# Layer 1 attention of a two-layer post-norm network: q and k turned in fp32 two heads at a time and split behind the turn, scores in 64-row tiles, row maximum written negated

## The chip, the cores and the metric

The kernel runs on one core of a Trainium2 chip. The metric is the device time of one execution in microseconds, from the first instruction to the last. Lower is better. Three executions of the kernel before took 630.36, 634.5 and 637.96 us, median 634.5.

A core has four engines that compute, each with its own in-order queue: TensorE (PE in the profile, its weight loads PEld), VectorE (DVE), ScalarE (ACT) and GpSimd (POOL). SyncE (SP) issues transfers. Engines wait for each other through semaphores. TensorE writes to PSUM, which has eight banks of 128 x 512 fp32 values here.

## The reference, cut to what matters

Two layers, each an attention and a feed-forward part with residual and layer norm, on x of shape (2, 512, 256). The change concerns the attention of layer 1: 32 query heads and 8 key/value heads of 64 values, so four query heads share a key head, rotary embedding, RMS norm of q and k, and a causal window of 64 positions.

```python
q, k, v = split(x @ w_qkv.T)           # 32, 8 and 8 heads of 64
q, k = rms_norm(q) * q_norm_w, rms_norm(k) * k_norm_w
q, k = q * cos + rot_half(q) * sin, k * cos + rot_half(k) * sin
scores = q @ k.T / sqrt(64)            # kept where 0 <= q_pos - k_pos < 64
out = softmax(scores) @ v
y = out @ w_out.T
```

The result is fp32. The kernel keeps its precision in TensorE's fast fp32r type by splitting a value into a high part, rounded to fp32r, and a low part, the remainder, and summing high x high, high x low and low x high.

## The kernel before

One program list, `STEPS`, sets the order of the work on every engine. Each engine's block walks through the list and does its own part of each step, so an instruction is never moved past one ahead of it in its queue. The order is: layer 0 attention, layer 0 feed-forward (`ffn`), layer 1 attention, layer 1 feed-forward.

**Passes.** Layer 1 attention works on 16 items, one for each batch and key head (`NIT`). It is a software pipeline of 22 passes. In pass n an engine does the steps of its list (`TENSOR_PASS`, `SCALAR_PASS`, `VECTOR_PASS`, `GPSIMD_PASS`), and an entry (name, behind, part) works on item n - behind. Three passes are done early, inside the layer 0 feed-forward. Passes 16 to 21 also carry the weight chunks of layer 1's feed-forward.

**An item** goes through these steps:
- `proj1` (x times w_qkv, four tiles t of 128 rows). PE writes 384 columns, and ScalarE copies them to `qkv_rows` (L853); VectorE copies tile 0 (L1143).
- `squares` on ScalarE, `square_sums` on VectorE (L1104), `rms_inverses` on GpSimd (L1281, L1282).
- `cosines` on VectorE (L1098), `sines` on GpSimd (two products, L1273), `rope_sums` on VectorE (L1111), which also tells GpSimd that `rope_sin_part` is free for the next sines. `normed` multiplies by the inverse and writes `roped` (L1120).
- `rows_high` on ScalarE (L889, L890) and `rows_low` on GpSimd (L1256, L1259) split q and k while positions are still on the partitions.
- `turn1k`, `turn1q` turn them on PE with an fp32r identity (L581): high and low of one head stand side by side, so one turn gives the high in rows 0 to 63 and the low in rows 64 to 127. ScalarE copies q to `q_stack` (L871) and k's high part twice into `k_stack` (L866, L867); VectorE copies k's low part twice (L1129, L1130).
- `scores1(k, c)`, c = 0 to 3: a bank first gets the mask (64-row bf16 matmul, L607), then eight matmuls over 128 rows (L616), which sum high and low of q against k's high and k's low.
- `maxima` on VectorE: a reduction (L1147), and a product by -1/8 of its 128x4 result (L1148) behind a wait for the first. `exps` on ScalarE: four exponentials with scale 1/8 and bias `minus_max`, each with its row sum (L877).
- `probs` on VectorE: reciprocal (L1135) and product (L1136). `turn_p` on PE (L624) with a copy on ScalarE (L894). `pv1` on PE (L638), ScalarE takes the high part (L899), VectorE the low (L937).
- `out1` on PE with w_out (L391 to L393); `wout` splits the chunk of w_out on ScalarE (L781) and GpSimd (L1228).

**Banks.** `claim` hands out banks 0 to 5 in a ring and makes PE wait until the bank's former contents have been read.

Of the kernel before, what the change touches and what calls it, by code (L numbers as in the profile page):

```python
# [1396 lines left out]
```

## Time and profile before

| | |
|---|---|
| three executions | 630.36, 634.5, 637.96 us |
| profiled execution | 634.5 us, span of its instructions 634.5 us |
| PE busy | 573.6 us (90%) |
| VectorE busy | 471.7 us (74%) |
| ScalarE busy | 385.9 us (61%) |
| GpSimd busy | 326.3 us (51%) |
| mean granted TensorE clock | 0.925 |

Busy time is the union of an engine's instructions. For matmuls it is a rough figure: they are pipelined and each record contains its latency. The granted clock is the share of TensorE's 2.4 GHz, and it has two levels, 1.0 and 0.5 (1.2 GHz). From about 200 to 545 us the kernel is in the layer 1 attention.

### The profile page before, as it was taken

How to read it: one execution, taken by the hardware profiler on the slowest of the kernel's cores; microseconds unless marked ns; L12 is line 12 of the kernel's file. 1: busy time of each engine (PE TensorE's matmuls, PEld its weight loads, DVE VectorE, ACT ScalarE, POOL GpSimd, SP SyncE). 2: the span in 40 equal slices, each digit the busy share in tenths (PEclk: the TensorE clock that was granted, in tenths of full speed). 3: DMA queues.
4: the chain of work that ended last, by engine and by line, in shares of the span. 5: the costliest groups of instructions: out<-in, count | busy, mean ns of one | idle time of the engine just before them, and what ended most of it. 6: DMA issues, size and time to landing. Idle time of an engine off the chain costs nothing.

```text
span 634.5 us, 11068 instructions
## 1 busy us (share of the span) xinstructions
PE 573.6 (90%) x3912; PEld 480.4 (76%) x3912; DVE 471.7 (74%) x786; ACT 385.9 (61%) x1020; POOL 326.3 (51%) x197
## 2 busy tenths in 40 slices
PE   3687988899999689999999999799999999899994
PEld 3444664688889678888888898688987787788883
DVE  4757777674455899999999999989998753363444
ACT  2555666415344378888888888758886665532230
POOL 2868665303423986666876666565759431230000
PEclk9878999899999788999999999989996765999997
DMA  8211001041310000000000000001011001000010
GB/s 305 77 38 33 3 1 34 2 147 54 92 33 1 1 1 18 1 19 18 18 19 18 2 18 19 18 1 35 18 35 51 27 24 52 34 1 1 1 34 33
DMA packets 8886, 21.10 MB, mean 33 GB/s; under 512 B 1280, under 2 KB 2944, under 8 KB 8704
## 3 DMA queue, kind: packets, MB, share of 16 engines
q1 hardware_dynamic: 8832, 20.40, 9.9%
q8 instruction: 32, 0.52, 0.3%
q14 instruction: 22, 0.18, 0.1%
HBM read 19.35 MB, written 1.05 MB: 32 GB/s over the span
## 4 chain that ended last, share of the span: by engine, by line
PE 45%; DVE 35%; issue 9%; ACT 4%; POOL 3%; DMA 1%; DVEq 1%; POOLq 0%; SPq 0%; ACTq 0%
PE psum L391 9%; PE psum L393 9%; PE psum L392 9%; DVE row_max L1147 5%; PE psum L616 4%; DVE rope_cos_part L1098 3%; DVE square_sums L1104 3%; DVE rope_cos_part L1111 3%; DVE roped L1120 3%; PE psum L467 3%; DVE probs L1136 3%; PE psum L450 2%; DVE out_t_low L937 2%; PE psum L638 2%; DVE minus_max L1148 2%
## 5 line engine op out<-in xcount | busy, mean ns | idle before, releaser
L877 ACT ACTIVATE probs<-psum,minus_max 128x128 f32<-128x128 f32 x256 | 90.5, 368 | 33.5 <-DVE minus_max L1148 33.4
L1273 POOL TENSOR_TENSOR rope_sin_part<-qkv_rows,sin_weighted 128x640 f32<-128x640 f32 x32 | 67.1, 2114 | 81.1 <-DVE rope_cos_part L1111 67.5
L616 PEld LDWEIGHTS psum<-k_stack,q_stack 128*128 128x128 f32 x512 | 71.6, 216 | 16.8 <-issue 16.8
L616 PE MATMUL psum<-k_stack,q_stack 128*128 128x128 f32 (+1 forms) x512 | 81.2, 308 | 0.0
L1282 POOL TENSOR_TENSOR rms_inverse<-rms_inverse,minus_half 128x20 f32<-128x20 f32 x16 | 58.7, 3668 | 1.3
L1237 POOL TENSOR_TENSOR weights_t<-weights_t,causal_block 128x512 f32<-128x512 f32 x32 | 45.3, 1437 | 23.7 <-DVE weights_t L981 18.6
L848 ACT CAST hidden_high<-hidden 128x512 fp32r<-128x512 f32 x32 | 19.8, 620 | 60.7 <-DVE hidden L1059 60.7
L1147 DVE TENSOR_REDUCE row_max<-psum 128x4 f32<-128x512 f32 x64 | 43.6, 682 | 12.9 <-PE psum L616 12.5
L877 ACT ACTIVATION_READ_ACCUMULATOR probs<-psum,minus_max 128x1 f32 x256 | 52.7, 206 | 0.0
L391 PE MATMUL psum<-x_t_high,ug_high 128*128 128x512 f32 x128 | 51.5, 402 | 0.0
L392 PE MATMUL psum<-x_t_low,ug_high 128*128 128x512 f32 x128 | 50.8, 396 | 0.0
L393 PE MATMUL psum<-x_t_high,ug_low 128*128 128x512 f32 x128 | 50.7, 396 | 0.0
L1148 DVE TENSOR_SCALAR minus_max<-row_max 128x4 f32<-128x4 f32 x64 | 47.0, 734 | 2.2
L1250 POOL TENSOR_SCALAR ln_var_eps<-ln_mean_var 128x4 f32<-128x4 f32 x8 | 1.8, 227 | 90.4 <-DVE ln_mean_var L1016 90.4
L391 PE MATMUL psum<-qkv_high,x_t_high 128*128 128x384 f32 x128 | 47.4, 371 | 0.5 <-DVE out_t_low L937 0.5
L1136 DVE TENSOR_TENSOR probs<-probs,prob_inverse 128x512 f32<-128x512 f32 x64 | 44.3, 692 | 2.2
L393 PE MATMUL psum<-qkv_high,x_t_low 128*128 128x384 f32 x128 | 44.1, 345 | 0.0
L392 PE MATMUL psum<-qkv_low,x_t_high 128*128 128x384 f32 x128 | 44.1, 345 | 0.0
L391 PE MATMUL psum<-wout_high,out_t_high 128*128 128x256 f32 x128 | 39.7, 310 | 3.5 <-DVE x_rows L1010 3.5
L624 PE MATMUL psum<-identity,probs 128*128 128x128 f32 x256 | 39.0, 288 | 3.9 <-DVE probs L1136 2.4
L581 PE MATMUL psum<-identity_r,q_rows_high_low 128*128 128x128 f32 x256 | 35.7, 281 | 6.3 <-DVE k_stack L1130 5.1
L1256 POOL TENSOR_TENSOR q_rows_high_low<-roped,q_rows_high_low 128x1024 fp32r<-128x1024 f32 x16 | 39.2, 2450 | 2.9 <-ACT k_rows_high_low L890 2.8
(159 smaller groups left out, 1667.5 us busy)
## 6 DMA issues: line engine op xcount, KB each, us to landing
raw_chunks<-in_ug SPq DMA_DIRECT2D x8, 512.0 KB, 3.6
raw_chunks<-in_wout SPq DMA_DIRECT2D x16, 256.0 KB, 2.7
raw_chunks<-in_qkv SPq DMA_DIRECT2D x8, 384.0 KB, 3.2
raw_chunks<-in_x SPq DMA_DIRECT2D x2, 512.0 KB, 5.1
raw_chunks<-in_w SPq DMA_DIRECT2D x2, 512.0 KB, 5.8
raw_chunks<-in_sel SPq DMA_DIRECT2D x2, 512.0 KB, 7.1
down_tree<-in_down SPq DMA_DIRECT2D x1, 1024.0 KB, 9.2
x_rows<-in_x_rows SPq DMA_DIRECT2D x2, 512.0 KB, 5.7
```

Source lines behind the costliest of these rows:

```text
L391: nc.tensor.matmul(o, ah_, bh_, start=first, stop=False, **kw)
L392: nc.tensor.matmul(o, ah_, bl_, start=False, stop=False, **kw)
L393: return nc.tensor.matmul(o, al_, bh_, start=False, stop=last, **kw)
L616: mm = nc.tensor.matmul(o[:, at:at + k1 - k0], qst[:, hp, qb, :], kst[:, k % 2, z, k0:k1], start=False, stop=z == 1, skip_group_check=True)
L877: e = nc.scalar.activation(pr[:, c, q, :], o[:, q * P:(q + 1) * P], ACT.Exp, bias=negm[:, c, q:q + 1], scale=float(HD1) ** -0.5, accum_out ...
L1136: nc.vector.tensor_tensor(pr[:, c], pr[:, c], pinv[:, c, :].rearrange("p (q a) -> p q a", a=1).to_broadcast([P, 4, P]), ALU.mult).then_inc ...
L1147: link(nc.vector.tensor_reduce(mx[:, c, :], o.rearrange("p (q w) -> p q w", q=4), AX.X, ALU.max))
L1148: nc.vector.tensor_scalar(negm[:, c, :], mx[:, c, :], -float(HD1) ** -0.5, None, ALU.mult).then_inc(mx_done[c], 1)
L1237: nc.gpsimd.tensor_tensor(w, w, tri[:].rearrange("p (a q) -> p a q", a=1).to_broadcast([P, HG, P]), ALU.mult).then_inc(w_mask, 1)
L1256: nc.gpsimd.tensor_tensor(qhl[:, :, :, 1, :], qn[:, :, 0:REP * HD1].rearrange("p t (h d) -> p t h d", h=REP), qhl[:, :, :, 0, :].bitcast(F ...
L1273: last = nc.gpsimd.tensor_tensor(ov[:, :, :, z, :], rv[:, :, :, 1 - z, :], sv[:, :, :, z, :], ALU.mult)
L1282: nc.gpsimd.tensor_tensor(r, r, half[:], ALU.pow).then_inc(rr_done, 1)
```

## The change

Where q and k are split changes. `normed` now writes k twice side by side (so `roped` has 384 values for each row instead of 320) in a first operation, and q in a second. PE turns these fp32 rows directly, two heads in one transpose, with k's turn giving k in both row halves. Only behind the turn are they split, ScalarE writing the high part (fp32r) and VectorE the low part, by subtraction from PSUM. `rows_high` and `rows_low` are gone.

`scores1` now has two parts instead of four. Each fills two banks, one for each of the two heads of a pair, from rows 0 to 63 and from rows 64 to 127, with three matmuls (high-high, high-low, low-high) over 64 rows. The factor 1/8 moves from the exponential to the tables for q. The reduction for the row maximum writes the negated maximum directly, so the 128x4 product is gone. `proj1(0, 0)`'s copy moves from VectorE to ScalarE. The order of the steps in all four lists is new.

```diff
+GN = GW + HD1
-TENSOR_PASS = [("turn1k", 4), ("out1", 6, 0), ("turn_p", 5, 0), ("turn_p", 5, 1), ("turn1q", 4, 0),
-    ("turn_p", 5, 2), ("proj1", 1, 1), ("turn1q", 4, 1), ("turn1q", 4, 2), ("turn1q", 4, 3), ("turn_p", 5, 3),
-    ("scores1", 4, 0), ("pv1", 5, 0), ("scores1", 4, 1), ("proj1", 1, 2), ("scores1", 4, 2), ("scores1", 4, 3),
-    ("out1", 6, 1), ("pv1", 5, 1), ("proj1", 1, 3), ("proj1", 0, 0)]
-SCALAR_PASS = [("turn1k", 4), ("squares", 2), ("turn_p", 5, 0), ("turn_p", 5, 1), ("turn1q", 4, 0), ("turn_p", 5, 2),
-    ("proj1", 1, 1), ("turn1q", 4, 2), ("turn1q", 4, 1), ("turn1q", 4, 3), ("turn_p", 5, 3), ("wout", 5),
-    ("rows_high", 3), ("pv1", 5, 0), ("exps", 4, 0), ("proj1", 1, 2), ("exps", 4, 1), ("exps", 4, 2), ("pv1", 5, 1),
-    ("exps", 4, 3), ("proj1", 1, 3)]
-VECTOR_PASS = [("turn1k", 4), ("probs", 5, 3), ("values1", 2), ("rope_sums", 3), ("normed", 3), ("maxima", 4, 0),
-    ("square_sums", 2), ("maxima", 4, 1), ("maxima", 4, 2), ("pv1", 5, 0), ("cosines", 2), ("maxima", 4, 3),
-    ("probs", 4, 0), ("probs", 4, 1), ("probs", 4, 2), ("pv1", 5, 1), ("proj1", 0, 0)]
-GPSIMD_PASS = [("rms_inverses", 3), ("sines", 2), ("wout", 5), ("rows_low", 3)]
+TENSOR_PASS = [("turn1k", 4), ("turn1q", 4, 0), ("turn1q", 4, 1), ("turn_p", 5, 0), ("turn_p", 5, 1), ("out1", 6, 0),
+    ("proj1", 1, 1), ("scores1", 4, 0), ("pv1", 5, 0), ("turn_p", 5, 2), ("turn_p", 5, 3), ("proj1", 1, 2),
+    ("scores1", 4, 1), ("out1", 6, 1), ("pv1", 5, 1), ("proj1", 1, 3), ("proj1", 0, 0)]
+SCALAR_PASS = [("turn1k", 4), ("turn1q", 4, 0), ("turn1q", 4, 1), ("turn_p", 5, 0), ("turn_p", 5, 1), ("squares", 2),
+    ("proj1", 1, 1), ("exps", 4, 0), ("pv1", 5, 0), ("exps", 4, 1), ("turn_p", 5, 2), ("turn_p", 5, 3), ("wout", 5),
+    ("proj1", 1, 2), ("exps", 4, 2), ("pv1", 5, 1), ("exps", 4, 3), ("proj1", 1, 3), ("proj1", 0, 0)]
+VECTOR_PASS = [("turn1k", 4), ("turn1q", 4, 0), ("turn1q", 4, 1), ("probs", 5, 3), ("values1", 2), ("square_sums", 2),
+    ("maxima", 4, 0), ("maxima", 4, 1), ("pv1", 5, 0), ("rope_sums", 3), ("probs", 4, 0), ("normed", 3),
+    ("probs", 4, 1), ("maxima", 4, 2), ("maxima", 4, 3), ("pv1", 5, 1), ("cosines", 2), ("probs", 4, 2)]
+GPSIMD_PASS = [("rms_inverses", 3), ("sines", 2), ("wout", 5)]
...
             def turn1k(k):
-                pe.wait_ge(identr_set, 1)
-                pe.wait_ge(rows_hi, k + 1)
-                pe.wait_ge(rows_lo, k + 1)
+                pe.wait_ge(qn_done, k + 1)
                 o, done = claim(("turn1k", k))
                 for t in range(TT):
-                    mm = turned(o[:, t * P:(t + 1) * P], khl[:, t, :, :])
+                    mm = nc.tensor.transpose(o[:, t * P:(t + 1) * P], qn[:, t, REP * HD1:GN], ident[:])
                 mm.then_inc(done, 1)
-            def turn1q(k, t):
-                o, done = claim(("turn1q", k, t))
-                for h in range(REP):
-                    mm = turned(o[:, h * P:(h + 1) * P], qhl[:, t, h, :, :])
+            def turn1q(k, hp):
+                o, done = claim(("turn1q", k, hp))
+                for t in range(TT):
+                    mm = nc.tensor.transpose(o[:, t * P:(t + 1) * P], qn[:, t, hp * P:(hp + 1) * P], ident[:])
                 mm.then_inc(done, 1)
...
+                banks = [claim(("scores1", k, 2 * half_ + h2)) for h2 in range(2)]
+                rows = [slice(HD1 * h2, HD1 * (h2 + 1)) for h2 in range(2)]
+                for h2 in range(2):
+                    nc.tensor.matmul(banks[h2][0], eye2[rows[h2], :], wmask[rows[h2], half_, :], start=True, stop=False,
+                                     skip_group_check=True)
+                emptied(pe, ("turn1k", k), ("turn1q", k, 0), ("turn1q", k, 1))
+                n = k % 2
+                for q4 in range(4):
+                    qb = 4 * half_ + q4
+                    k0, k1 = max(0, (qb - 1) * WIN), (qb + 1) * WIN
+                    at = q4 * P + P - (k1 - k0)
+                    for z, (qt, kt) in enumerate(((qth, kth), (qth, ktl), (qtl, kth))):
+                        for h2 in range(2):
+                            o, done = banks[h2]
+                            mm = nc.tensor.matmul(o[:, at:at + k1 - k0], qt[rows[h2], n, qb, :, :].rearrange("p a w -> p (a w)"),
+                                                  kt[rows[h2], n, k0:k1], start=False, stop=z == 2,
+                                                  skip_group_check=True)
...
+                high(("turn1k", k), kth[:, k % 2, :])
...
+                nc.scalar.copy(qth[:, k % 2, :, hp, :], o.rearrange("p (qb w) -> p qb w", qb=NQ)).then_inc(hi_done, 1)
...
             def normed(k):
...
-                    dve.wait_ge(rows_lo, k)
+                    filled(dve, ("turn1k", k - 1))
+                    for hp in range(2):
+                        filled(dve, ("turn1q", k - 1, hp))
+                inverse = rr[:, k % 2, :].rearrange("p (t h a) -> p t h a", t=TT, a=1)
                 nc.vector.tensor_tensor(
-                    qn[:].rearrange("p t (h d) -> p t h d", d=HD1), rot1[:].rearrange("p t (h d) -> p t h d", d=HD1),
-                    rr[:, k % 2, :].rearrange("p (t h a) -> p t h a", t=TT, a=1).to_broadcast([P, TT, REP + 1, HD1]),
-                    ALU.mult).then_inc(qn_done, 1)
+                    qn[:, :, REP * HD1:GN].rearrange("p t (a d) -> p t a d", a=2),
+                    rot1[:, :, REP * HD1:GW].rearrange("p t (a d) -> p t a d", a=1).to_broadcast([P, TT, 2, HD1]),
+                    inverse[:, :, REP:REP + 1, :].to_broadcast([P, TT, 2, HD1]), ALU.mult)
+                nc.vector.tensor_tensor(
+                    qn[:, :, 0:REP * HD1].rearrange("p t (h d) -> p t h d", d=HD1),
+                    rot1[:, :, 0:REP * HD1].rearrange("p t (h d) -> p t h d", d=HD1),
+                    inverse[:, :, 0:REP, :].to_broadcast([P, TT, REP, HD1]), ALU.mult).then_inc(qn_done, 1)
...
+                low(("turn1k", k), ktl[:, k % 2, :], kth[:, k % 2, :])
+            def turn1q(k, hp):
+                low(("turn1q", k, hp), qtl[:, k % 2, :, hp, :], qth[:, k % 2, :, hp, :],
+                    lambda o: o.rearrange("p (qb w) -> p qb w", qb=NQ))
...
-                link(nc.vector.tensor_reduce(mx[:, c, :], o.rearrange("p (q w) -> p q w", q=4), AX.X, ALU.max))
-                nc.vector.tensor_scalar(negm[:, c, :], mx[:, c, :], -float(HD1) ** -0.5, None,
-                                        ALU.mult).then_inc(mx_done[c], 1)
+                nc.vector.tensor_reduce(negm[:, c, :], o.rearrange("p (q w) -> p q w", q=4), AX.X, ALU.max,
+                                        negate=True).then_inc(mx_done[c], 1)
```

## Rows read from the trace of the kernel before

**Rows 1.** Busy time, five even passes: PE, PEld, DVE, ACT, POOL, PEclk, DMA, GB/s.

```profile
280.68:376.30 95.62, 95.03 (x763) 83.91 (x761) 93.26 (x140) 80.34 (x256) 66.77 (x35) 1.00 0.05 15
```

**Rows 2.** VectorE's groups, 280.68 to 376.30: count, busy us, mean ns, idle before.

```profile
L1148 DVE TENSOR_SCALAR minus_max<-row_max 128x4 f32<-128x4 f32 x20 | 16.5, 824 | 0.7
L1136 DVE TENSOR_TENSOR probs<-probs,prob_inverse 128x512 f32<-128x512 f32 x20 | 13.8, 692 | 0.7
L1147 DVE TENSOR_REDUCE row_max<-psum 128x4 f32<-128x512 f32 x20 | 13.6, 680 | 0.2
...
L1120 DVE TENSOR_TENSOR roped<-rope_cos_part,rms_inverse 128x1280 f32<-128x1280 f32 x5 | 7.5, 1492 | 0.2
...
L937 DVE TENSOR_TENSOR out_t_low<-psum,out_t_high 128x512 fp32r<-128x512 f32 x10 | 6.8, 680 | 0.0
L1130 DVE CAST k_stack<-psum 64x512 fp32r<-64x512 f32 x5 | 3.5, 694 | 0.1
...
L1143 DVE COPY qkv_rows<-psum 128x384 f32<-128x384 f32 x5 | 2.7, 546 | 0.0
```

**Rows 3.** VectorE in order of time, one pass: start us, us, what.

```profile
280.68 1.49 DVE L1111 TENSOR_TENSOR rope_cos_part<-rope_cos_part,rope_sin_part 128x1280 f32<-128x1280 f32 x1
...
288.51 1.72 DVE L1148 TENSOR_SCALAR minus_max<-row_max 128x4 f32<-128x4 f32 x1
...
292.95 0.17 DVE L1135 RECIPROCAL prob_inverse<-prob_sums 128x4 f32<-128x4 f32 x1
...
293.77 0.17 DVE L1135 RECIPROCAL prob_inverse<-prob_sums 128x4 f32<-128x4 f32 x1
...
299.81 1.49 DVE L1111 TENSOR_TENSOR rope_cos_part<-rope_cos_part,rope_sin_part 128x1280 f32<-128x1280 f32 x1
```

**Rows 4.** ScalarE in order of time, the same pass.

```profile
284.99 0.58 ACT L899 CAST out_t_high<-psum 128x512 fp32r<-128x512 f32 x1
285.47 0.37 ACT L877 ACTIVATE probs<-psum,minus_max 128x128 f32<-128x128 f32 x1
...
286.85 0.49 ACT L853 COPY qkv_rows<-psum 128x384 f32<-128x384 f32 x1
```

**Rows 5.** GpSimd in order of time, the same pass.

```profile
282.34 4.28 POOL L1273 TENSOR_TENSOR rope_sin_part<-qkv_rows,sin_weighted 128x640 f32<-128x640 f32 x2 [5.54 <-DVE rope_cos_part L1111]
286.58 1.27 POOL L1228 TENSOR_TENSOR wout_low<-raw_chunks,wout_high 128x512 fp32r<-128x512 f32 x1
287.82 2.38 POOL L1256 TENSOR_TENSOR q_rows_high_low<-roped,q_rows_high_low 128x1024 fp32r<-128x1024 f32 x1
```

**Rows 6.** VectorE in order of time, an early pass.

```profile
208.71 2.79 DVE L1120 TENSOR_TENSOR roped<-rope_cos_part,rms_inverse 128x1280 f32<-128x1280 f32 x1 [0.73 <-POOL rms_inverse L1282]
```

**Rows 7.** GpSimd in order of time, the same early pass.

```profile
208.58 4.33 POOL L1273 TENSOR_TENSOR rope_sin_part<-qkv_rows,sin_weighted 128x640 f32<-128x640 f32 x2
```

**Rows 8.** VectorE in order of time, in layer 0.

```profile
25.52 3.41 DVE L956 TENSOR_TENSOR x_t_low<-raw_chunks,x_t_high 128x1024 fp32r<-128x1024 f32 x1 [2.22 <-ACT x_t_high L781]
```

**Rows 9.** GpSimd in order of time, in layer 0.

```profile
25.49 2.34 POOL L1204 TENSOR_TENSOR down_tree<-down_tree 128x1024 f32<-128x1024 f32 x1
```

**Rows 10.** PE in order of time, layer 0 scores, 64-row matmuls in both row halves.

```profile
89.83 0.76 PE L450 MATMUL psum<-qk_stacks 64*128 64x512 f32 x4
90.52 1.71 PE L467 MATMUL psum<-weights_t,v_and_ones 128*32 128x512 f32 x16
```

**Rows 11.** PE in order of time, the same pass as Rows 3.

```profile
281.17 1.11 PE L616 MATMUL psum<-k_stack,q_stack 128*128 128x64 f32 x8
...
298.15 1.11 PE L581 MATMUL psum<-identity_r,q_rows_high_low 128*128 128x128 f32 x9
```

**Rows 12.** The chain that ended last, in the tail: start us, us, what.

```profile
499.65 0.70 DVE k_stack L1130
...
523.42 0.71 DVE k_stack L1130
```

**Rows 13.** Busy time by stages, in the tail; columns as in Rows 1.

```profile
503.00:507.00 4.00, 4.00 (x26) 3.44 (x25) 2.24 (x1) 0.67 (x2) 2.90 (x2) 0.50 0.01 3
```

More of the change, by code:

```diff
@@ L227, in post_ln_two_layers @@
         with ExitStack() as s:
-            qn = place(s, "roped", [TT, GW], F32)
-            qhl = place(s, "q_rows_high_low", [TT, REP, 2, HD1], F32R)
-            khl = place(s, "k_rows_high_low", [TT, 2, HD1], F32R)
+            qn = place(s, "roped", [TT, GN], F32)
             wol = place(s, "wout_low", [2, 2, C], F32R)
-            qst = place(s, "q_stack", [2, NQ, P], F32R)
-            kst = place(s, "k_stack", [2, 2, T], F32R)
+            qth = place(s, "q_t_high", [2, NQ, 2, WIN], F32R)
+            qtl = place(s, "q_t_low", [2, NQ, 2, WIN], F32R)
+            kth = place(s, "k_t_high", [2, T], F32R)
+            ktl = place(s, "k_t_low", [2, T], F32R)
             pr = place(s, "probs", [4, 4, P], F32)
@@ new lines, in scores1 @@
+                for q4 in range(4):
[8 more added lines that the diff above has]
+                                                  skip_group_check=True)
+                            if q4 == 3 and z == 2:
+                                mm.then_inc(done, 1)
@@ L862, in turn1k @@
             def turn1k(k):
-                o, _ = take(act, ("turn1k", k))
-                hi_no["turn1k", k] = len(hi_no) + 1
-                nc.scalar.copy(kst[0:HD1, k % 2, 0, :], o[0:HD1])
-                nc.scalar.copy(kst[HD1:P, k % 2, 0, :], o[0:HD1]).then_inc(hi_done, 1)
-            def turn1q(k, t):
-                o, done = take(act, ("turn1q", k, t))
-                nc.scalar.copy(*to_qst(o, t)).then_inc(done, 1)
+                high(("turn1k", k), kth[:, k % 2, :])
+            def turn1q(k, hp):
+                o, _ = take(act, ("turn1q", k, hp))
+                hi_no["turn1q", k, hp] = len(hi_no) + 1
+                nc.scalar.copy(qth[:, k % 2, :, hp, :], o.rearrange("p (qb w) -> p qb w", qb=NQ)).then_inc(hi_done, 1)
             def exps(k, c):
@@ L1069, in rope_tables @@
                     for t in range(TT):
-                        last = nc.vector.tensor_tensor(
-                            tab[:, t, :].rearrange("p (h d) -> p h d", h=REP + 1),
-                            nw[:, z, :].rearrange("p (h d) -> p h d", h=REP + 1),
-                            ctab[:, z, t, :].rearrange("p (a d) -> p a d", a=1).to_broadcast([P, REP + 1, HD1]),
-                            ALU.mult)
+                        angle = ctab[:, z, t, :].rearrange("p (a d) -> p a d", a=1)
+                        for h0, h1, by in ((0, REP, float(HD1) ** -0.5), (REP, REP + 1, 1.0)):
+                            cols = slice(h0 * HD1, h1 * HD1)
+                            last = nc.vector.scalar_tensor_tensor(
+                                out=tab[:, t, cols].rearrange("p (h d) -> p h d", d=HD1),
+                                in0=nw[:, z, cols].rearrange("p (h d) -> p h d", d=HD1), scalar=by,
+                                in1=angle.to_broadcast([P, h1 - h0, HD1]), op0=ALU.mult, op1=ALU.mult)
                 last.then_inc(tabs_done, 1)
@@ L1155, in pv1 @@
                     lambda o: o.rearrange("p (q hp w) -> p q hp w", q=4, hp=2))
-            in_pass = dict(proj1=proj1, turn1k=turn1k, pv1=pv1, maxima=maxima, probs=probs, cosines=cosines,
+            in_pass = dict(turn1k=turn1k, turn1q=turn1q, pv1=pv1, maxima=maxima, probs=probs, cosines=cosines,
                            square_sums=square_sums, normed=normed, values1=values1, rope_sums=rope_sums)
@@ L1171, in tree_step @@
             def tree_step():
-                for name in ("identity", "scale_ug", "scale_dp"):
+                for name in ("scale_ug", "scale_dp"):
                     dve.wait_ge(const_in[name], 16)
-                nc.vector.tensor_copy(identr[:], ident[:]).then_inc(identr_set, 1)
                 nc.vector.tensor_scalar(scale_ug[:], scale_ug[:], float(C) ** -0.5, None, ALU.mult)
```

75 lines of the change are left out of this document (13 added, 62 removed).

## The prediction, made before the changed kernel ran

> **What bounds the kernel now.** I read the busy time by stages first, then VectorE's groups in the layer 1 attention, then one pass of that stage engine by engine. The stage is a software pipeline of 22 passes. Between 280.68 and 376.30 us five passes run alike at the full TensorE clock, 19.12 us each, VectorE busy 93.26 of 95.62 us and PE 95.03 [rows 1]; the same step of VectorE, `rope_sums`, starts at 280.68 and 299.81 [rows 3]. The reader should see two engines without slack, ScalarE at 80.3 and GpSimd at 66.8. PE's busy time counts overlapping records, so it is an upper bound.
>
> Then one oddity: `minus_max`, a 128x4 operation, takes 0.824 us on average, more than a reduction of 128x512 at 0.680 [rows 2]. At 288.51 it takes 1.72 us, until GpSimd's operation that began at 287.82 and took 2.38 is over [rows 3, 5]. So some VectorE operations with both ends in SBUF wait until a running GpSimd operation is through. A `tensor_tensor` with two SBUF inputs does too: `roped`, 1.49 us otherwise, took 2.79 when GpSimd's sine product had started 0.13 us before it [rows 2, 6, 7], and a split at 25.52 took 3.41 because GpSimd had started at 25.49 [rows 8, 9]. In the first of these the two sine products took 4.33 us. Free of waits they take about 2.9: in the even pass 4.28 us, of which the first 1.36 (282.34 to 283.70) are under `roped` [rows 5]. So in the early pass they alternated: product, `roped`, product [rows 6, 7]. Reductions and PSUM operands show no such wait.
>
> **VectorE, per pass.** From 19.12 us go four `minus_max`, 4 x 0.824 = 3.30; the copy of `proj1(0,0)`, 0.55 (ScalarE takes it); two `k_stack` casts, 1.39. Added are three subtractions PSUM minus SBUF; their like is `out_t_low` at 0.680, of which some 0.07 overlaps the next: +1.85. `normed` becomes 128x512 and 128x1024: 0.69 and, between 0.69 for 512 and 1.49 for 1280, 1.23, less overlap, against 1.49: +0.3 [rows 2]. Work left: 16.0 us.
>
> But the queue order adds waits. ScalarE now runs `exps(0)` before the high part of `pv1(0)`, and VectorE's `pv1` low part stands right behind `maxima(0)`, `maxima(1)`. From the end of the first maximum: 0.09 to the exponentials, 1.38 for four of them (285.47 to 286.85), 0.58 for the high part, together 2.05 us [rows 4]; VectorE has only the second maximum, 0.60, to fill it. Idle 1.45 us. The same pattern comes again with `maxima(2)`, `maxima(3)`: 2.9 us a pass, so 18.9. In the kernel before, the first high part goes ahead of the exponentials, and VectorE has three `probs` ahead of the second low part.
>
> Then the port. `rope_sums` is now followed by `probs(0)`, `normed` (two operations), `probs(1)`: four products of two SBUF inputs in a row. `rope_sums` also releases GpSimd's two sine products, and `wout_low` (1.27 us [rows 5]) is queued behind them. Before, `roped` stood there alone and was first in. Now a reciprocal comes first (0.17 us; reciprocal and product together move the queue on by 0.82, from 292.95 to 293.77 [rows 3]), so the product starts some 0.23 us behind the end of `rope_sums`. GpSimd starts 0.17 behind it: 282.34 against 280.68 + 1.49 [rows 3, 5]. I take it that they alternate: VectorE waits about 1.35, 1.4 and 1.15 us for the three GpSimd operations: 3.9 us. Bounds: nothing, if VectorE is first and keeps the port over consecutive operations; 4.3, the three whole. I take 3.9, as the one row where both waited shows alternation. VectorE's pass: 16.0 + 2.9 + 3.9 = 22.8 us, **3.7 us more**. The rope tables take eight operations more and the identity copy is gone, both in layer 0, where VectorE has gaps: 0, and 2 to 3 us without them.
>
> The Trainium skill, "SBUF — State Buffer", section on SBUF's two separate sides, calls the shared pair an exclusive lock, granted for the whole instruction to whoever starts first. It doesn't say who gets it when both wait; with VectorE keeping it the sum would be that of the second rival.
>
> **PE.** The turn of q falls from 16 matmuls (nine take 1.11 us [rows 11]) to 8 transposes, k stays at 4: about -0.9. The scores: 32 matmuls at 0.13 us (eight take 1.11 with the last one's latency [rows 11]) become 48 on 64 rows. Half-height matmuls in the two row halves run at the same time: four of 512 columns take 0.69 us to the next group, 0.17 each, under the 0.21 that 512 columns need at 2.4 GHz [rows 10]. So 24 pairs at 0.11 to 0.13, about 2.9 instead of 4.2, and masks in pairs, -0.6. From 19.0 PE falls to some 16.3 us, under VectorE; if halves did not overlap, it would be 19, still under 22.8. This is hidden.
>
> **ScalarE and GpSimd.** ScalarE loses four `q_stack`, two `k_stack` and two row casts and gains three casts and a copy, so its 16.1 us can only fall; GpSimd loses `rows_low`, whose larger part takes 2.38 us [rows 5]. Both lie beside VectorE: 0. If VectorE had no waits, PE would be next.
>
> **A queue of banks.** Claims go round six banks, 17 to a pass. The last turn of q may only be written once `exps(3)` of the pass before is done; from there PE has turns 0.5, two turns of probabilities 1.0, `out1` 1.4, `proj1` 1.1, scores 1.8: 5.8 us at full clock. VectorE gets to its first maximum about 6.7 us behind `exps(3)`. Hidden by 0.9 us.
>
> **Sum.** Passes 5 to 16 are of this kind: 12 x 3.7 = +44. Pass 4: +3. In the tail (no projections) `k_stack` comes at 499.65 and 523.42, 23.8 us apart [rows 12], PE at half clock between (0.50 at 503 to 507 [rows 13]). There eight scores matmuls take about 1.9, and the new scores save some 3 us of PE. Pass 17 keeps all of VectorE's work: 22.8, no gain; pass 18 about 21, -3; pass 19 about 16, -6: -9. 634.5 + 44 + 3 - 9 = 672.5, forecast **672 us**. The profiled execution's 634.5 is also the median of the three runs, which spread from 630.4 to 638.0, so within 1% (6 us) nothing can be told from no change.
>
> **Rivals.**
> 1. *The clock falls in every pass* (slower still). Waiting for `exps(3)` behind a late `maxima(3)`, PE stands about 4 us. The clock fell in the tail after a stand between the q turns. At half clock for part of PE's 5.8 us path, 2.5 more less the 0.9 in hand: +1.6 on 13 passes, 693 us. For: the longer stand. Against: in the five even passes it never fell with as many projections. Chance 0.15. The Trainium skill, "TensorE: Matmul & The Clock Gate", Part 4, says that transposes don't count as activity for the clock; 20 in a row now open a pass. The trace doesn't separate this.
> 2. *VectorE keeps the port, or gets there first.* 18.9 us a pass: 13 x -0.2 = -3, and the tail -13 (pass 17 gains 3 and pass 18 4 instead of 0 and 3): **618 us**, the other side. It decides at the start of `probs(0)`: if that starts ahead of the sine product, this holds. For: the starts lie only 0.06 us apart by estimate. Against: the alternation, and 25.49 against 25.52. Chance 0.16.
> 3. *Only the first sine product blocks.* 18.9 + 1.4 = 20.3: +1.2 x 13 = 15, tail -11: 638. Chance 0.16.
> 4. *The waits of step order don't bind either*, and the pass is the busiest engine's 16.4: -2.7 x 13 = -35, tail -13: 587. For: the work really is removed. Against: in-order queues, and both waits are certain by the rows. Chance 0.10.
>
> **Chances and range.** My case 0.43. Faster by over 1% (under 628): rivals 2 and 4 and a little of 3, 0.28. Within 1%: most of 3, 0.14. Slower: 0.58. The range leaves out rival 4 and the outer half of the first and goes from 612 to 698; the likeliest case alone is 660 to 685 (a pass of 21.8 to 23.8).
>
> **What would show it.** A pass of 22 to 24 us between consecutive `rope_sums`. `probs` on average well above 0.69 us and the two parts of `roped` near 2.1 and 2.4; `minus_max` straight from PSUM at 0.68. VectorE idle about 1.45 us ahead of `out_t_low`, twice a pass, released by ScalarE. Score matmuls starting in pairs, thousandths of a us apart. In the tail, passes under 22 us. I am wrong if `probs` stays at 0.69 (rival 2), if only the first of each pass is long (rival 3), or if VectorE has no waits ahead of `out_t_low` (rival 4); the granted clock between 280 and 376 us tells rival 1.

## The result and the profile after

The kernel after the change takes **686.1 us** (median of four executions, 678.8 to 688.5), the kernel before 633.0 (median of four, 630.4 to 638.0): ratio 1.081, 95% interval 1.073 to 1.089. It is slower, as forecast; 672 had been predicted, in a range of 612 to 698. The profiled execution took 688.5 us, its span is 686.7. Some executions of one kernel ran over 1.5% longer than its fastest, at a lower granted clock (three of nine for e2, five of ten for e4 below), and medians and ratios leave them out.

First the busy time of the page, and below it the same for four passes of the stage, to be set beside [rows 1]:

```profile
PE 556.4 (81%) x4040; PEld 473.3 (69%) x4040; DVE 477.6 (70%) x745; ACT 345.1 (50%) x956; POOL 278.5 (41%) x165
```

```profile
301.60:397.01 95.41, 76.10 (x640) 68.68 (x640) 77.31 (x101) 54.35 (x190) 41.23 (x20) 0.86 0.04 12
```

The stretch is as long as before but holds four passes instead of five: 23.88 us each against 19.12. No engine is full any more: PE is busy for 76.1 of 95.4 us and VectorE for 77.3, of which, as the next rows show, 3.6 us a pass are waits inside its operations. Work went, waits came. VectorE's groups in that stretch (count, busy us, mean ns, idle before and who ended it) answer to [rows 2]:

```profile
L1116 DVE TENSOR_TENSOR probs<-probs,prob_inverse 128x512 f32<-128x512 f32 x16 | 14.6, 912 | 0.5
L1100 DVE TENSOR_TENSOR roped<-rope_cos_part,rms_inverse 128x1024 f32<-128x1024 f32 x4 | 10.3, 2567 | 0.0
L1122 DVE TENSOR_REDUCE minus_max<-psum 128x4 f32<-128x512 f32 x16 | 10.3, 681 | 3.3 <-PE psum L606 3.3
L1096 DVE TENSOR_TENSOR roped<-rope_cos_part,rms_inverse 128x512 f32<-128x512 f32 x4 | 8.2, 2047 | 0.0
L908 DVE TENSOR_TENSOR out_t_low<-psum,out_t_high 128x512 fp32r<-128x512 f32 x9 | 6.2, 692 | 14.3 <-ACT out_t_high L870 14.3
...
L908 DVE TENSOR_TENSOR k_t_low<-psum,k_t_high 128x512 fp32r<-128x512 f32 x4 | 2.8, 692 | 1.3 <-ACT k_t_high L751 1.3
```

Two things are to be seen: `probs` and both parts of `roped` are long, and 14.3 us of idle stand ahead of nine `out_t_low`. One pass of VectorE in order of time (start us, us, what; in brackets the idle before and its releaser) shows both. It answers to [rows 3].

```profile
349.26 1.48 DVE L1084 TENSOR_TENSOR rope_cos_part<-rope_cos_part,rope_sin_part 128x1280 f32<-128x1280 f32 x1
350.66 0.17 DVE L1115 RECIPROCAL prob_inverse<-prob_sums 128x4 f32<-128x4 f32 x1
350.86 0.69 DVE L1116 TENSOR_TENSOR probs<-probs,prob_inverse 128x512 f32<-128x512 f32 x1
351.47 2.05 DVE L1096 TENSOR_TENSOR roped<-rope_cos_part,rms_inverse 128x512 f32<-128x512 f32 x1
353.44 2.57 DVE L1100 TENSOR_TENSOR roped<-rope_cos_part,rms_inverse 128x1024 f32<-128x1024 f32 x1
...
356.13 1.58 DVE L1116 TENSOR_TENSOR probs<-probs,prob_inverse 128x512 f32<-128x512 f32 x1
357.63 1.28 DVE L1122 TENSOR_REDUCE minus_max<-psum 128x4 f32<-128x512 f32 x2
360.48 0.69 DVE L908 TENSOR_TENSOR out_t_low<-psum,out_t_high 128x512 fp32r<-128x512 f32 x1 [1.58 <-ACT out_t_high L870]
...
363.72 0.69 DVE L908 TENSOR_TENSOR k_t_low<-psum,k_t_high 128x512 fp32r<-128x512 f32 x1 [0.33 <-ACT k_t_high L751]
...
369.65 1.29 DVE L1122 TENSOR_REDUCE minus_max<-psum 128x4 f32<-128x512 f32 x2 [0.85 <-PE psum L606]
372.52 0.69 DVE L908 TENSOR_TENSOR out_t_low<-psum,out_t_high 128x512 fp32r<-128x512 f32 x1 [1.59 <-ACT out_t_high L870]
373.13 1.48 DVE L1084 TENSOR_TENSOR rope_cos_part<-rope_cos_part,rope_sin_part 128x1280 f32<-128x1280 f32 x1
```

GpSimd in the same pass, the answer to [rows 5]:

```profile
350.91 4.02 POOL L1236 TENSOR_TENSOR rope_sin_part<-qkv_rows,sin_weighted 128x640 f32<-128x640 f32 x2 [13.37 <-ACT probs_t L865]
354.88 2.27 POOL L1200 TENSOR_TENSOR wout_low<-raw_chunks,wout_high 128x512 fp32r<-128x512 f32 x1
```

Read the two together. `probs` starts at 350.86, the sine product at 350.91. From then on the engines take turns: `roped` for k takes 2.05 instead of .69, `roped` for q 2.57 instead of 1.23, `probs(1)` 1.58 instead of .69, and GpSimd's operations are stretched too. This is what the prediction calls the port, and VectorE's price is 1.36 + 1.34 + .89 = 3.6 us a pass. The idles are 1.58 and 1.59 ahead of `out_t_low`, .85 ahead of the first maximum, .33 ahead of `k_t_low`. VectorE is busy for 19.3 us of a pass, which is 15.7 without the waits: 15.7 + 3.6 + 3.2 + .85 + .33 = 23.7, against the measured 23.88. The rest are small gaps between operations.

ScalarE shows why `out_t_low` is late (answer to [rows 4]): four exponentials, from 358.40, stand ahead of the cast.

```profile
358.40 0.37 ACT L859 ACTIVATE probs<-psum,minus_max 128x128 f32<-128x128 f32 x1 [6.58 <-DVE minus_max L1122]
...
359.79 0.60 ACT L870 CAST out_t_high<-psum 128x512 fp32r<-128x512 f32 x1
```

PE, finally. The score matmuls start two at a time, .11 us apart. And PE stands for 2.81 us ahead of the first turn of q, until `exps(2)` (from 358.40 to 359.90) gives its bank back, and .77 ahead of the second, until `exps(3)` has:

```profile
350.48 0.29 PE L606 MATMUL psum<-k_t_high,q_t_low 64*128 64x128 f32 x2
350.60 0.29 PE L606 MATMUL psum<-k_t_high,q_t_high 64*128 64x128 f32 x2
...
359.96 1.12 PE L586 MATMUL psum<-identity,roped 128*128 128x128 f32 x4 [2.81 <-ACT probs L859]
361.85 1.11 PE L586 MATMUL psum<-identity,roped 128*128 128x128 f32 x4 [0.77 <-ACT probs L859]
```

The granted clock is 0.86 in this stretch, where it was 1.00 before [rows 1]: in each pass it is at the lower level for 6.8 us, from about the end of that stand on.

**Where the 52 us are.** The `probs` of block 3 comes once in each pass, soon after its start. The first, the thirteenth and the last of the 16, first those of the kernel after, then those of before:

```profile
247.75 0.69 DVE L1116 TENSOR_TENSOR probs<-probs,prob_inverse 128x512 f32<-128x512 f32 x1
...
537.41 0.69 DVE L1116 TENSOR_TENSOR probs<-probs,prob_inverse 128x512 f32<-128x512 f32 x1
...
600.45 0.69 DVE L1116 TENSOR_TENSOR probs<-probs,prob_inverse 128x512 f32<-128x512 f32 x1
```

```profile
240.83 0.69 DVE L1136 TENSOR_TENSOR probs<-probs,prob_inverse 128x512 f32<-128x512 f32 x1
...
478.35 0.69 DVE L1136 TENSOR_TENSOR probs<-probs,prob_inverse 128x512 f32<-128x512 f32 x1
...
549.56 0.69 DVE L1136 TENSOR_TENSOR probs<-probs,prob_inverse 128x512 f32<-128x512 f32 x1
```

Up to the first: +6.9 us. The next twelve gaps: 289.7 against 237.5, +52.1. The last three gaps and the rest of the span: -6.9. Together 52.2 before rounding, which is 686.7 - 634.5.

Of these, 2.2 us are already there when layer 0 ends: its last `hidden` starts at 201.18 us, and at 199.01 before. That is no effect of the change that could be told. In the profiled executions of e1 to e3 and e5 to e10 below, whose layer 0 is that of the kernel after, the same operation starts anywhere between 194.01 (e9) and 201.27 us (e1), with a mean granted clock over the first 100 us of 0.95 in the early ones and 0.88 in the late ones. So differences of whole times of single executions hold up to 7 us of this, and passes are the better measure.

### The profile page after: what moved, and what is told of

Read it like the earlier page. It is cut to its first block and busy times, and to the rows that moved or that the text cites. A ratio compares the mean times of both kernels' runs of the same rounds, so it can differ in the third digit from the quotient of the medians.

```text
span 686.7 us, 11172 instructions
## 1 busy us (share of the span) xinstructions
PE 556.4 (81%) x4040; PEld 473.3 (69%) x4040; DVE 477.6 (70%) x745; ACT 345.1 (50%) x956; POOL 278.5 (41%) x165
## 3 DMA queue, kind: packets, MB, share of 16 engines
HBM read 19.35 MB, written 1.05 MB: 30 GB/s over the span
## 5 line engine op out<-in xcount | busy, mean ns | idle before, releaser
L586 PE MATMUL psum<-identity,roped 128*128 128x128 f32 x128 | 31.0, 398 | 39.0 <-ACT probs L859 39.0
L908 DVE TENSOR_TENSOR out_t_low<-psum,out_t_high 128x512 fp32r<-128x512 f32 x36 | 24.8, 691 | 54.2 <-ACT out_t_high L870 53.9
L1116 DVE TENSOR_TENSOR probs<-probs,prob_inverse 128x512 f32<-128x512 f32 x64 | 56.3, 880 | 2.2
L616 PE MATMUL psum<-identity,probs 128*128 128x128 f32 x256 | 48.2, 348 | 7.2 <-ACT probs L859 7.2
L586 PEld LDWEIGHTS psum<-identity,roped 128*128 128x128 f32 x128 | 21.7, 202 | 45.8 <-ACT probs L859 45.8
L838 ACT COPY qkv_rows<-psum 128x384 f32<-128x384 f32 x64 | 32.2, 506 | 33.7 <-PE psum L388 20.9
L1122 DVE TENSOR_REDUCE minus_max<-psum 128x4 f32<-128x512 f32 x64 | 41.0, 681 | 11.3 <-PE psum L606 11.3
L616 PEld LDWEIGHTS psum<-identity,probs 128*128 128x128 f32 x256 | 40.3, 183 | 11.6 <-issue 11.5
L386 PE MATMUL psum<-wout_high,out_t_high 128*128 128x256 f32 x128 | 46.8, 366 | 0.0
L606 PE MATMUL psum<-k_t_high,q_t_high 64*128 64x128 f32 (+1 forms) x256 | 41.7, 314 | 5.8 <-DVE q_t_low L908 5.8
```

What stands on the lines that cost most here:

```text
L386: nc.tensor.matmul(o, ah_, bh_, start=first, stop=False, **kw)
L586: mm = nc.tensor.transpose(o[:, t * P:(t + 1) * P], qn[:, t, hp * P:(hp + 1) * P], ident[:])
L606: mm = nc.tensor.matmul(o[:, at:at + k1 - k0], qt[rows[h2], n, qb, :, :].rearrange("p a w -> p (a w)"), kt[rows[h2], n, k0:k1], start=Fals ...
L616: mm = nc.tensor.transpose(o[:, q * P:(q + 1) * P], pr[:, c, q, :], ident[:])
L1116: nc.vector.tensor_tensor(pr[:, c], pr[:, c], pinv[:, c, :].rearrange("p (q a) -> p q a", a=1).to_broadcast([P, 4, P]), ALU.mult).then_inc ...
L1122: nc.vector.tensor_reduce(negm[:, c, :], o.rearrange("p (q w) -> p q w", q=4), AX.X, ALU.max, negate=True).then_inc(mx_done[c], 1)
```

## The experiments

Ten kernels. All ratios are to the kernel before, run beside them (medians 633.1 to 634.1 us). A pass is counted from one `rope_sums` to the next, in the stretch from about 301 to 397 us of one profiled execution.

| kernel | median us | ratio, 95% interval | pass us |
|---|---|---|---|
| after | 686.1 | 1.081 [1.073, 1.089] | 23.88 |
| e1: high part of pv1 first | 645.0 | 1.021 [1.015, 1.027] | 20.16, one 21.51 |
| e2: rope_sums early | 635.6 | 1.005 [1.000, 1.010] | 20.5 to 20.6 |
| e3: e1 and e2 | 644.0 | 1.019 [1.012, 1.026] | 20.8 to 22.1 |
| e4: before, maximum negated | 619.9 | 0.978 [0.973, 0.984] | 18.3 to 18.7 |
| e5: after, clock kept up | 675.7 | 1.068 [1.063, 1.074] | 22.92 |
| e6: VectorE's order | 610.1 | 0.963 [0.958, 0.968] | 18.2 to 18.6 |
| e7: scores not paired | 687.7 | 1.087 [1.082, 1.091] | 22.9 to 24.5 |
| e9: e6, wout high later | 608.5 | 0.960 [0.955, 0.965] | 18.4 to 18.6 |
| e8: e9, probs(3) earlier | 605.2 | 0.956 [0.950, 0.963] | 17.8 to 18.6 |
| e10: e8, wout elsewhere | 601.0 | 0.947 [0.939, 0.955] | 17.2 to 18.5 |

### The two waits, one by one

**e1** changes ScalarE's list:

```
-    ("exps", 4, 0), ("pv1", 5, 0), ("exps", 4, 1),  ...  ("exps", 4, 2), ("pv1", 5, 1), ("exps", 4, 3)
+    ("pv1", 5, 0), ("exps", 4, 0), ("exps", 4, 1),  ...  ("pv1", 5, 1), ("exps", 4, 2), ("exps", 4, 3)
```

> The changed kernel with one move on ScalarE alone: in each half pass the high part of pv1 stands ahead of the exponentials instead of behind the first four. My theory: VectorE's two stands of 1.6 us ahead of out_t_low (3.2 us of a pass of 23.9) go, the port waits of 3.6 us stay: a pass of 20.5 to 21.2 us, 645 to 655 us in all. Rival, PE's half-clock stretch sets the pass: the stand moves to row maxima waiting for the scores, a pass of 22.5 to 23.9, 675 to 686 us.

It took 645.0 us. The idle ahead of `out_t_low` fell to .4 us in ten, `roped` stayed at 2.05 and 2.57. The idle of 3.2 us went, and with it, in all passes of the stretch but one, the .85 ahead of the first maximum; the idle ahead of `k_t_low` grew from .33 to .93. Sum: 23.88 - 3.2 - .85 + .6 = 20.4, measured 20.16; an operation that starts without an idle also overlaps the one before it by some .08 us, three times here. The idle that the prediction had counted is real and was on the path.

**e2** changes VectorE's list:

```
-    ("values1", 2), ("square_sums", 2), ("maxima", 4, 0), ("maxima", 4, 1), ("pv1", 5, 0), ("rope_sums", 3), ("probs", 4, 0),
+    ("values1", 2), ("rope_sums", 3), ("square_sums", 2), ("maxima", 4, 0), ("maxima", 4, 1), ("pv1", 5, 0), ("probs", 4, 0),
```

> The changed kernel with one move on VectorE alone: rope_sums stands ahead of square_sums, so that the reductions, which read PSUM or one SBUF tensor, run while GpSimd does its two sine products and wout_low. My theory: the port waits in probs and roped (3.6 us a pass) fall to under 1 us, the stands ahead of out_t_low stay at 3.2: a pass of 20.8 to 21.5, 650 to 658 us. Rival, the products are slow for another reason (their shape, or the k rows written twice): roped stays at 1.9 and 2.5 us and nothing changes, 686.

It took 635.6 us, less than the 650 to 658 expected. `roped` fell to .69 and 1.22, its time without waits, and one `probs` of four kept 1.56 us, beside `wout_low`. So 2.7 of the 3.6 us of port waits went, and the .85 ahead of the first maximum too, because VectorE comes to it later: 23.88 - 2.7 - .85 = 20.3, measured 20.47. `rope_sums` also first runs at 201.4 us instead of 212.3. Of these 10.9 us, 6.6 are layer 0, which was quicker in this execution (its last `hidden` at 194.55). The other 4.3 are the order, and this I had left out. In the kernel after, the second `square_sums` stands ahead of it and waits for GpSimd's power:

```profile
201.18 0.75 DVE L1030 SCALAR_TENSOR_TENSOR hidden<-psum,scale_ug,silu_gate 128x512 f32<-128x512 f32 x1 [6.26 <-PE psum L388]
...
210.89 1.49 DVE L1077 TENSOR_REDUCE square_sums<-squares 128x20 f32<-128x1280 f32 x1 [2.92 <-POOL rms_inverse L1245]
212.30 1.48 DVE L1084 TENSOR_TENSOR rope_cos_part<-rope_cos_part,rope_sin_part 128x1280 f32<-128x1280 f32 x1
```

**e3** does both.

> Both moves at once (high part of pv1 ahead of the exponentials, rope_sums ahead of square_sums). My theory: VectorE keeps 16 us of work and about 1 us of waits, PE needs 16.3 and stands less, so the clock stays up more: a pass of 17 to 18.5 us, 595 to 615 us in all, faster than both kernels. Rival, the clock still falls once a pass: 19 to 20 us, 625 to 640.

A miss, by 29 us and more: 644.0 us, slower than e2 alone and above even the 625 to 640 of its rival. No port wait is left (`probs` .692 on average), yet the pass takes 20.8 to 22.1. ScalarE, then VectorE, of this kernel in order of time:

```profile
310.90 1.11 ACT L865 COPY probs_t<-psum 128x512 f32<-128x512 f32 x2
311.84 0.69 ACT L766 CAST wout_high<-raw_chunks 128x512 fp32r<-128x512 f32 x1
312.36 0.55 ACT L838 COPY qkv_rows<-psum 128x384 f32<-128x384 f32 x1
317.06 0.59 ACT L870 CAST out_t_high<-psum 128x512 fp32r<-128x512 f32 x1 [4.15 <-PE psum L628]
```

```profile
313.15 1.29 DVE L1122 TENSOR_REDUCE minus_max<-psum 128x4 f32<-128x512 f32 x2
317.75 0.69 DVE L908 TENSOR_TENSOR out_t_low<-psum,out_t_high 128x512 fp32r<-128x512 f32 x1 [3.31 <-ACT out_t_high L870]
```

PE of the same stretch:

```profile
311.19 0.39 PE L595 MATMUL psum<-window_mask,eye_twice 64*128 64x512 bf16 x2 [2.81 <-ACT probs L859]
...
315.92 1.09 PE L628 MATMUL psum<-probs_t,v_rows 128*64 128x128 f32 x16
```

Both maxima are done at 314.44, so the exponentials could start by then. But the cast now stands ahead of them, and it waits for pv1's matmuls, which PE starts at 315.92, behind the scores and `out1` that it could not begin before 311.19. ScalarE stands 4.15 us and VectorE 3.31. Some 1.2 us of this is the clock: behind PE's stand of 2.81 us the granted clock is .53 from 313.5 to 316.0, and `out1` takes 2.83 us (from 313.09), where it took 1.62 in the kernel after at the full clock (351.71 to 353.33). e1's cure had cost ScalarE the same kind of stand (29.6 us in ten of them), unseen while VectorE was slow. It moved the wait to ScalarE.

### The part that is a gain by itself

**e4** takes the kernel before and writes the maximum negated, with the factor 1/8 in the tables for q:

```
-                link(nc.vector.tensor_reduce(mx[:, c, :], ..., ALU.max))
-                nc.vector.tensor_scalar(negm[:, c, :], mx[:, c, :], -float(HD1) ** -0.5, None, ALU.mult)...
+                nc.vector.tensor_reduce(negm[:, c, :], ..., ALU.max, negate=True)...
```

> The kernel before with one part of the change: the row maximum is written negated by the reduction, the factor 1/8 moves to the tables of q, and the 128x4 product is gone. VectorE loses 3.7 us of 19.1 a pass. If VectorE alone bounds that kernel: 15.5 to 16.5 a pass, near 600 us. My theory: PE, with some 18.8 us of matmuls, is next at once: 18.7 to 19.0 a pass, 628 to 633. Rival, the port waits pass to the next products of VectorE: no change in VectorE's time, 633 to 636.

Its median is 619.9 us, 2.2% under before (interval 1.6 to 2.7%) and under the 628 to 633 expected. The windows row of five passes, and `cosines` in VectorE's order of time:

```profile
301.60:395.20 93.60, 93.60 (x762) 83.90 (x761) 80.62 (x121) 81.28 (x257) 69.48 (x37) 1.00 0.06 16
```

```profile
305.90 2.26 DVE L1099 TENSOR_TENSOR rope_cos_part<-qkv_rows,cos_weighted 128x1280 f32<-128x1280 f32 x1
```

PE is busy for the whole stretch and VectorE for 80.6 of 93.6 us, with 8.7 us of idle ahead of maxima, waiting for the scores. Here the pass is PE's, at 18.3 to 18.7 us; my estimate of PE's own time before, 19.0, was too high. Of the waits on GpSimd one was handed on: `cosines` takes 2.26 instead of 1.48.

### The clock

**e5** lets PE multiply zeros into the open output accumulator in its stand ahead of the turn of q:

```
             def turn1q(k, hp):
+                if hp == 0 and ... acc1:
...
+                    for _ in range(22):
+                        nc.tensor.matmul(acc1[0][0][:, 0:256], zeros[:, 0:P], zeros[:], start=False, stop=False, ...)
                 o, done = claim(("turn1q", k, hp))
```

> The kernel after, with 22 matmuls of zeros (128x256, bf16) added to the open output accumulator ahead of the turn of the first two q heads, so that TensorE works through its 2.8 us stand of every pass; the output is unchanged. If the half-clock stretch of 6.8 us a pass is what makes the first maximum late (.85 us) and k's low half wait (.33 us), the stretch vanishes and the pass falls from 23.88 to 22.7-22.9: 670-675 us. If the clock lies beside the chain (VectorE's queue alone sets the pass), the clock is kept and the time stays at 684-688. If the added matmuls themselves delay the turns (they are in TensorE's queue), 690-700.

675.7 us, just above the 670 to 675 expected, and a pass of 22.92 as expected: the .96 us is the .85 ahead of the first maximum and little else. Window and maxima of the same stage:

```profile
301.60:393.30 91.70, 83.03 (x742) 76.13 (x743) 76.92 (x101) 54.16 (x188) 40.93 (x21) 0.91 0.04 13
```

```profile
L1129 DVE TENSOR_REDUCE minus_max<-psum 128x4 f32<-128x512 f32 x16 | 10.2, 679 | 0.0
```

The idle ahead of the maxima is 0.0 instead of 3.3 us. The clock still falls at times (0.91), and the .33 ahead of `k_t_low` stays (1.3 us in four). By the medians the slower clock cost 10 us of the 53, by way of late scores. The two profiled executions say 8.7: that much shorter is all that lies behind the first `rope_sums` (465.7 against 474.4 us), and another 3.5 us are layer 0, in which no zeros are multiplied.

### The pairs of score matmuls

**e7** puts the second head's matmuls behind the first's:

```
-                for q4 in range(4): ... for z, (qt, kt) in enumerate(...): for h2 in range(2): <matmul>
+                for h2 in range(2): for q4 in range(4): ... for z, (qt, kt) in enumerate(...): <matmul>
```

> The kernel after, with the score matmuls of the second head all behind those of the first instead of alternating with them; same matmuls, same banks. If the two 64-row tiles of a pair work at once (two matmuls per .11 us), each now takes .11 us or more alone: TensorE +2.6 us a pass, the first head's bank is done as early as before, the second 1.3 us later, of which the first maximum (.6) covers half: +.7 to +1.4 us a pass, 694-702 us. If the pair never ran at once, or the chain has slack there: 684-688.

687.7 us, no change that can be told from 686.1. One head's matmuls alone:

```profile
315.10 0.27 PE L606 MATMUL psum<-k_t_high,q_t_low 64*128 64x128 f32 x1
315.21 0.27 PE L606 MATMUL psum<-k_t_high,q_t_high 64*128 64x128 f32 x1
315.32 0.27 PE L606 MATMUL psum<-k_t_low,q_t_high 64*128 64x128 f32 x1
```

They too start .11 us apart, one where the pair was two. So the two row halves do work at once, and pairing saves about 1.05 us of PE in each half, 2.1 a pass (the 24 take 2.42 us here, from 314.41 to 316.83, and 1.37 in pairs). In the passes it brings nothing, because they are VectorE's: ten of them in a row take 232.8 us here and 232.5 in the kernel after. Outside them the two profiled executions differ, and the equal whole times hide it: layer 0 was 7.0 us shorter in e7's and the part behind the ten passes 5.4 us longer. Two single executions can't say whether the missing pairs have a part in the latter.

### A version that beats both

**e6** fills each idle ahead of `out_t_low` with VectorE's own work and lets GpSimd's sines run beside reductions:

```
-    ("values1", 2), ("square_sums", 2),
-    ("maxima", 4, 0), ("maxima", 4, 1), ("pv1", 5, 0), ("rope_sums", 3), ("probs", 4, 0), ("normed", 3),
-    ("probs", 4, 1), ("maxima", 4, 2), ("maxima", 4, 3), ("pv1", 5, 1), ("cosines", 2), ("probs", 4, 2)]
+    ("values1", 2), ("rope_sums", 3),
+    ("maxima", 4, 0), ("maxima", 4, 1), ("square_sums", 2), ("pv1", 5, 0), ("probs", 4, 0), ("normed", 3),
+    ("probs", 4, 1), ("maxima", 4, 2), ("maxima", 4, 3), ("cosines", 2), ("pv1", 5, 1), ("probs", 4, 2)]
```

> The kernel after, with VectorE's order alone changed: rope_sums ahead of the maxima (so GpSimd's sines run beside maxima and square_sums, which take no part in the port waits), square_sums between the second maximum and out_t_low of half 0, cosines between the fourth maximum and out_t_low of half 1, so that each idle of 1.6 us ahead of out_t_low has VectorE work in it. ScalarE's order stays, so it does not wait for pv1 as it did when its orders were changed. If the pass is VectorE's work plus idle plus port waits, 16.0 + .9 (one probs against wout_low) = 16.9, with TensorE's 16.3 near: pass 17-18.5, 585-610 us, below the 626 of the kernel before with the negated maximum. If a ring through TensorE and ScalarE sets the pass once VectorE is free (as with both changes together, 20.8-22.1): 630-645. If the clock still falls for 3.4 us in a pass: 605-630.

610.1 us: 11% faster than after, by the order of one engine's list alone, and 3.7% faster than before. The pass of 18.5 is longer than the 16.9 of the sum. VectorE's rows show what is left: .89 beside `wout_low`, two idles of up to .5, and 1.2 ahead of `k_t_low`.

```profile
339.33 0.69 DVE L908 TENSOR_TENSOR out_t_low<-psum,out_t_high 128x512 fp32r<-128x512 f32 x1 [0.19 <-ACT out_t_high L870]
...
342.69 1.58 DVE L1116 TENSOR_TENSOR probs<-probs,prob_inverse 128x512 f32<-128x512 f32 x1
```

**e8 and e9** take up the two large ones. Both put ScalarE's wout high one copy later; e8 also moves `probs(3)`:

```
 SCALAR_PASS:
-    ("turn_p", 5, 3), ("wout", 5), ("proj1", 1, 2),
+    ("turn_p", 5, 3), ("proj1", 1, 2), ("wout", 5),
 VECTOR_PASS, e8 alone:
-    ("turn1q", 4, 1), ("probs", 5, 3), ("values1", 2),  ...  ("probs", 4, 2)]
+    ("turn1q", 4, 1), ("values1", 2),  ...  ("probs", 4, 2), ("probs", 4, 3)]
```

> The run before (VectorE's order changed) with two more moves. ScalarE's wout high goes one copy later, so that GpSimd's wout_low starts just after probs(1) instead of just before it (probs(1) took 1.58 against .69: .88 us a pass). And probs of block 3 goes ahead of k's low half, into VectorE's idle of 1.16 us there. If VectorE's queue sets the pass of 18.4-18.6: minus .88 and minus .86, near 16.9-17.3 with TensorE's 16.3 close behind: 588-600 us. If TensorE or a ring through ScalarE takes over at once, 603-611. Above 611 if the later wout high or the earlier turn of probs holds up something else.

> Of these two moves the one of wout high alone. GpSimd and VectorE come for probs(1) within .05 us of each other, so it tells whether the price of .88 us a pass hangs on that order: if VectorE comes first and keeps its .69, the pass falls from 18.5 to 17.6 and the time to 597-602 us; if GpSimd still comes first, no change, 608-612.

e9 came out on the second side of its expectation: 608.5 us, which is e6's within its noise, and the pass stayed. GpSimd, then VectorE:

```profile
339.18 1.29 POOL L1200 TENSOR_TENSOR wout_low<-raw_chunks,wout_high 128x512 fp32r<-128x512 f32 x1 [2.98 <-DVE roped L1100]
```

```profile
339.23 1.79 DVE L1116 TENSOR_TENSOR probs<-probs,prob_inverse 128x512 f32<-128x512 f32 x1
```

GpSimd is still first, by .05 us, and as it has the whole operation before it, `probs` now waits 1.1 instead of .89. e8's second move did work: 17.8 us in most passes, 605.2 us. That is not the 588 to 600 of its theory, and the wait that stayed is 1.1 us a pass of it.

**e10** moves wout right away from those products:

```
 SCALAR_PASS:
-    ("turn1k", 4), ("turn1q", 4, 0), ("turn1q", 4, 1),  ...  ("proj1", 1, 2), ("wout", 5),
+    ("turn1k", 4), ("turn1q", 4, 0), ("wout", 5), ("turn1q", 4, 1),  ...  ("proj1", 1, 2),
-GPSIMD_PASS = [("rms_inverses", 3), ("sines", 2), ("wout", 5)]
+GPSIMD_PASS = [("rms_inverses", 3), ("wout", 5), ("sines", 2)]
```

> The kernel e8_two_more_moves with wout taken out of the stretch of the roped multiplications: ScalarE's wout high between the high halves of the two q blocks, GpSimd's wout_low ahead of the sines, where VectorE works on k_t_low, q_t_low and v_rows, which showed no port wait in any run. If the last port wait goes (probs(1) 1.78 back to .69, 1.09 us a pass) against some .25 us of idle ahead of the second q_t_low: pass 17.8 to 16.9-17.0, TensorE's 16.3 close: 590-597 us. If GpSimd's wout_low meets rope_sums and moves the wait there, or TensorE's stands take over: 600-607.

601.0 us, 5.3% under the kernel before, but above the 590 to 597 of its theory. Its interval overlaps e8's. Behind the first `rope_sums` its profiled execution takes 393.8 us against e8's 398.8. The waits of `probs` are gone; only a copy of `v_rows`, now beside `wout_low`, takes .39 us instead of .29:

```profile
L1117 DVE TENSOR_TENSOR probs<-probs,prob_inverse 128x512 f32<-128x512 f32 x22 | 15.2, 692 | 0.8
```

```profile
301.60:397.00 95.40, 87.81 (x866) 80.86 (x866) 86.53 (x136) 72.32 (x259) 40.85 (x26) 0.98 0.05 16
```

The shortest passes take 17.2 us. The one of 18.5 (297.18 to 315.71) goes with the clock: the granted clock is .54 from 306 to 309 us, the matmuls of `pv1` take 1.77 us instead of 1.09, and VectorE stands 1.40 ahead of `out_t_low` where it stood .19. PE had stood 1.26 us ahead of the scores. One pass later, behind the same stand, the clock stayed at 1.00.

## Why the prediction was right, and by how much it missed

**The mechanism** was the one forecast: VectorE's queue sets the pass, with idles ahead of `out_t_low` and with waits on GpSimd, and PE's savings are hidden. e1 shows the idles by itself, e2 the waits, and e7 that PE's savings are hidden in the passes.

**VectorE's work**, 16.0 us a pass: 15.7 by its busy time. The maximum straight from PSUM takes .681, `roped` .69 and 1.22 without waits.

**The idle**, 1.45 twice: measured 1.58 and 1.59. Right.

**The port**, 3.9 us: measured 3.6, but not quite in the way described. I had GpSimd start first and `probs(0)` wait. `probs(0)` was first, by .05 us, and took .69; the three waits fell on `roped`, `roped` and `probs(1)`. By the mark that I had set for rival 2, the start of `probs(0)` ahead of the sine product, that rival should have held. It did not: being first bought one operation, and after it the engines took turns. The mark was badly chosen; alternation carried the price, not the first start. The Trainium skill, "SBUF — State Buffer", in its section on the two separate sides, describes an exclusive lock for whole instructions. These rows agree with that, and they add the turn-taking between two waiting engines. They part from it at GpSimd's `rms_inverse` (128x20, 3.53 us): in e6 it ran from 344.42 to 347.95, and `cosines`, a product of two SBUF operands, began beside it at 345.39 and took its 1.48 us.

**The clock** was rival 1, at .15, with +1.6 us a pass. It joined the main case instead of replacing it. PE stood 2.81 us instead of "about 4", the clock was at the lower level for 6.8 us of each pass, and the price was .85 to 1 us (e5). The term that this moved is the queue of banks: from the end of `exps(3)` to the end of the scores PE took 7.9 us (361.79 to 369.65), not 5.8, so that instead of hiding by 0.9 it came .85 too late. My argument against it, that it never fell in the five even passes, rested on a PE without stands, which the change did away with. As to the transposes, e6 has the same list on PE and one pass of it (334.94 to 353.29) ran at a granted clock of 1.00 throughout: 20 of them in a row did not bring it down there.

**The terms.** Twelve passes at +3.7 = 44 were in fact +52.1 (4.3 each). An even pass is 4.8 longer, not 3.7, and .96 of the difference is the clock (e5). Pass 4 at +3 stands against +6.9 up to the first `probs` of block 3: 2.2 of it is layer 0, which varies by more than that from one execution to the next, 3.6 the way from there to the first `rope_sums`, where the second `square_sums` waited 2.92, and only 1.1 the pass itself. The tail at -9 stands against -6.9: pass 17 was 3.1 longer rather than even, passes 18 and 19 were 4.1 and 7.2 shorter (foreseen 3 and 6), and behind them came +1.3. So 8 + 4 + 2 make the 14 us between 672.5 and 686.7. That the total came within 14 us has some luck in it: the port and the work were put a little too high, and pass 4's +3 happened to cover part of a start that was not in the sum.

**The other rivals.** That the waits of step order don't bind (rival 4) fell with e1. That only the first sine product blocks (rival 3) fell with two long `roped` and a long `probs`. PE "under VectorE" held: with 2.1 us more of PE a pass in e7 the ten passes did not move. The claim that ScalarE and GpSimd lie beside the path held for their work, and not for their order: e1 took 41 us away by ScalarE's list alone.

## What to carry to other kernels

A change that takes work from a full engine has to be read together with the order of its queue. Here the same operations ran in 686 us in the order given and in 601 in the best order tried, 14% apart and on either side of the kernel before. Look in each list for the operation that waits, and put one of the engine's own that is ready in front of it; moving another engine's producer forward took 41 us away here (e1) but left a new wait on that engine, and two cures need not add up (e3). And keep VectorE's products of two SBUF operands away from GpSimd's large products: beside reductions and PSUM operands the same GpSimd work cost nothing (e6: the sines took 3.08 us beside two maxima and `square_sums` at their usual length).
